# Third cross-attention of a perceiver: the first group's keys made in gaps of the stages ahead and kept, variances from whole squares, wider weighing in the second

## The chip, the cores and the metric

The kernel runs on one NeuronCore of a Trainium2 chip. Its engines are TensorE (PE in the profile: matmuls, with PEld for its weight loads), VectorE (DVE), ScalarE (ACT), GpSimd (POOL) and SyncE (SP, which issues loads). Each works through its own queue in order; semaphores tie them together. Arrays lie in SBUF, results of matmuls in PSUM, which has 8 banks of 128 x 512 f32. The metric is the device time of one execution in microseconds (us), the median of a few.

## What is computed

A chain of twelve stages (0 to 11) on a latent `x` of 64 x 256 and a context of 6272 x 256: four rounds of cross-attention, self-attention and a feed-forward or expert layer, each added to `x`. Three stages matter here. Stage 3 (L1 cross-attention, integer-valued softmax weights), shortened:

```
q = _fq_sym(q * scale); k = _fq_sym(k); v = _fq_sym(v, axis=2)
attn = softmax(einsum('bhqd,bhkd->bhqk', q, k))        # 16 heads of 16
attn = _fq_unsigned(attn, axis=-1)                     # steps of max/255
out = einsum('bhqk,bhkd->bhqd', attn, v) @ Wp + bp
```

Stage 6 (L2 cross-attention, "the third"), shortened. `cond` is the context; 8 groups of keys of 128, 2 query heads for each:

```
ln_out = _ln(hidden_states, ln_w, ln_b)
q, k, v = fp8-rounded linears of ln_out;  q, k = _ln(q), _ln(k)
core = _gqa(q, k, v)                                   # over the 64 latents
qx = _ln(fp8-rounded linear of ln_out)
kx, vx = split(einsum('bsi,oi->bso', cond, w_kv_x))
kx = _ln(kx)                                           # per group, over 128
xout = _gqa(qx, kx, vx)                                # over the 6272 of cond
return fp8-rounded concat([core, xout]) @ wproj * scales
```

Stages 4 and 5 between them are a self-attention (16 heads of 16 over 64 latents) and a layer of 8 experts.

## The kernel before

Every engine has a function for each stage (`x1_tensor`, `x2_vector`, ...), and the order of its work is written out by hand; there is no scheduler. Where TensorE would wait, `busy(pe, n, b)` issues n matmuls of 128x512 in bf16 whose result nobody reads (line 500); tables `BUSY_NORM`, `BUSY_OUT`, `BUSY_MHA` say how many at which place.

**Stage 3** runs over 8 pairs of heads. For each, `scores` (L1845) writes four parts, VectorE copies them out with their maximum (L1930), ScalarE takes exponentials in 7 parts (L2008), TensorE turns each (`turn`, L1860: 7 transposes of 128x128 in bf16), ScalarE or VectorE copies the turned part (L1813), and TensorE multiplies it with the values (`weigh`, L1869: 7 matmuls of 128x32).

**Stage 4**: `mha_tensor` makes queries and keys (L640), turns them (L647), scores (L655), turns the probabilities in two halves (L666), and multiplies by the values (L674). ScalarE takes the two exponentials (L736) and copies the two halves (L739).

**Stage 6** begins with two norms and the fp8 rounding on VectorE. TensorE makes six blocks of heads (`block`, L2097), each in a bank of its own (0 to 5): block 0 and 1 the cross queries, 2 and 3 the core queries, 4 the core keys, 5 the core values. VectorE takes their moments (L2334) and normalises blocks 0 and 1 (L2347), ScalarE blocks 2 to 4 (L2591), TensorE turns each (`turn`, L2109), ScalarE scales them (L2598), and `constant` (L2115) makes a term of the scores. Then the 8 groups follow. The context is in 49 tiles of 128, 13 chunks of up to 4 tiles. For each chunk of a group: `keys` (L2153: the group's weights as stationary operand, 512 columns of context moving, 2 matmuls); ScalarE copies the keys (L2630) and squares them (L2637); VectorE takes from the square its high bf16 half, which leaves a low half (`low_half`, L2385); `variance` sums both over 128 rows, a column per tile, with 8 bf16 matmuls (L2165, L2166); VectorE reads it out (L2396), GpSimd takes the power -1/2 (L2717); `scores` (L2182) multiplies keys and query; VectorE scales by the inverse and adds the constant (L2408), and keeps a running maximum (L2420). In `step(scored, weighed, ahead)` one group is scored while the group before is weighed (`weigh`, L2192), and `change` stands between two steps: it takes the maximum over lanes and rows (`turn_top` L2199, `spread_top` L2204) and begins the next group's keys. The first step, `step(0, None, 1, ...)`, has nothing to weigh; the core attention (L2123, L2133, L2141 on TensorE; L2482 to L2490 on VectorE) is put between its chunks.

The context is reloaded for it by SyncE: `ctxT` (feature-major, for the keys) in two halves during and behind stage 3's scores, `ctxN` (row-major, for the weighing) behind stage 3, into the buffer `vals`. In stage 3 the upper half of `vals`, named `back`, holds the scores of every other pair.

## Time and profile before

| | us |
|---|---|
| median of 3 runs | 1125.19 (1125.15 to 1125.84) |
| the profiled execution | 1126.49, of which span 1124.7 |
| TensorE busy | 1032.3 (92%) |
| VectorE, ScalarE, GpSimd busy | 745.1, 400.2, 158.5 |
| stage 3, from its norm to the end of its projection | 296 to 413 |
| stage 4 | 414 to 432 |
| stage 5 | 433 to 458 |
| stage 6, norms and head | 458 to 491 |
| its six blocks: start of the first, start of the third | 465.75, 469.2 |
| stage 6, first group scored | 491 to 530 |
| first weighing of stage 6 | 539.90 |
| load of `ctxN`, from issue to landing | 23.1 |
| GpSimd's power -1/2, 128x4 elements | 1.32 |
| VectorE's wait for the query projection, start of stage 3 | 2.04 |
| granted clock in 396 to 400, 400 to 415, 415 to 418 | 0.83, 0.50, 0.88 |
| granted clock in 473.5 to 477.5, and in 528.5 to 535 | 0.57, 0.50 |

How to read it: the rows further down are lines of the profile. A row of time has its start, its length, the engine, the line of the kernel, what is written and read, and in brackets how long the engine had waited and for whom. Matmuls overlap in the pipeline, so the time that one costs in a stream is read from start to start. f32 matmuls appear as two records each.

### The profile page before, as it was taken

The page shows a single profiled execution, that of the slowest core. Times are in us where ns is not written, and L with a number is a line of the kernel's source. Part 1 is how long each engine was busy: PE and PEld are TensorE (multiplying, and loading weights), DVE is VectorE, ACT ScalarE, POOL GpSimd, SP SyncE. Part 2 cuts the span into 40 slices and gives each one's busy share as a digit, 9 for nine tenths or more (in the row PEclk, how much of TensorE's full clock was granted, in tenths as well). Part 3 has the DMA queues.
Part 4 walks back from the last instruction along what each step waited for, and adds up shares of the span by engine and source line. Part 5 has one row for each costly group of instructions (what it writes and reads, how often), then busy time and mean ns, then how long its engine had stood idle before and what let it go on. Part 6 is the DMA issues. An engine that isn't in the chain of part 4 may idle for free.

```text
span 1124.7 us, 22087 instructions
## 1 busy us (share of the span) xinstructions
PE 1032.3 (92%) x8292; PEld 685.0 (61%) x8308; DVE 745.1 (66%) x1957; ACT 400.2 (36%) x738; POOL 158.5 (14%) x148
## 2 busy tenths in 40 slices
PE   6999999998777778899999999999999998988888
PEld 4667766664345545355676767777777776744444
DVE  4767676777678835658677676767676767553244
ACT  1333333334279951053333333333333333111203
POOL 0000000001000010124232223222232222000000
PEclk9999999999989969998999999999999998989899
DMA  7101010011302057640000000000000001323430
GB/s 271 37 21 37 19 37 19 23 47 54 122 1 117 2 202 259 229 141 1 1 1 2 1 0 0 0 0 1 0 0 0 0 1 59 108 79 129 158 116 3
DMA packets 17962, 64.51 MB, mean 57 GB/s; under 512 B 1392, under 2 KB 8304, under 8 KB 14448
## 3 DMA queue, kind: packets, MB, share of 16 engines
q1 hardware_dynamic: 17472, 63.08, 15.7%
q8 instruction: 39, 0.64, 0.2%
q10 hardware_dynamic: 432, 0.64, 0.2%
q14 instruction: 19, 0.16, 0.0%
HBM read 63.65 MB, written 0.07 MB: 57 GB/s over the span
## 4 chain that ended last, share of the span: by engine, by line
PE 71%; DVE 12%; issue 8%; ACT 4%; POOL 3%; DMA 1%; SPq 0%; DVEq 0%; POOLq 0%
PE ps L2192 14%; PE ps L2153 12%; PE ps L1460 7%; PE ps L2182 7%; PE ps L1450 4%; PE ps L1471 4%; PE ps L1494 2%; PE ps L1506 2%; POOL x_sum L2717 2%; PE ps L1845 2%; ACT wide L2008 1%; DVE S L2408 1%; DVE S L1930 1%; ACT x_keys L1813 1%; PE ps L500 1%
## 5 line engine op out<-in xcount | busy, mean ns | idle before, releaser
L2192 PE MATMUL ps<-vals,S 128*128 128x257 f32 x784 | 187.3, 382 | 0.7 <-ACT S L2642 0.7
L2153 PE MATMUL ps<-keysT,row_biases_sb 128*128 128x512 f32 (+1 forms) x416 | 187.2, 576 | 0.1
L2717 POOL TENSOR_TENSOR x_sum<-x_max,consts 128x4 f32<-128x4 f32 (+1 forms) x104 | 133.9, 1287 | 325.1 <-DVE x_max L2396 325.1
L2408 DVE SCALAR_TENSOR_TENSOR S<-ps,x_sum,keysT 128x128 f32<-128x128 f32 x392 | 110.9, 344 | 72.6 <-PE ps L2192 64.2
L2192 PEld LDWEIGHTS ps<-vals,S 128*128 128x128 f32 x784 | 142.4, 191 | 18.6 <-issue 1.0
L2642 ACT ACTIVATE S<-S 128x512 f32<-128x512 f32 (+1 forms) x104 | 62.7, 606 | 219.4 <-DVE S L2443 218.8
L2182 PE MATMUL ps<-x_q,x_keys 128*128 128x128 f32 x784 | 113.2, 286 | 0.0
L2153 PEld LDWEIGHTS ps<-keysT,row_biases_sb 128*128 128x128 f32 x416 | 77.0, 193 | 57.2 <-issue 52.1
L2182 PEld LDWEIGHTS ps<-x_q,x_keys 128*128 128x128 f32 x784 | 95.6, 191 | 0.0
L1460 PE MATMUL ps<-ring,S 128*128 128x512 f32 x196 | 92.2, 593 | 1.9 <-DVE ps L1601 1.9
L2630 ACT COPY x_keys<-ps 128x512 f32<-128x512 f32 (+1 forms) x104 | 57.1, 549 | 66.0 <-PE ps L2182 34.2
L1574 ACT ACTIVATE S<-ps 128x2048 f32<-128x2048 f32 (+1 forms) x25 | 46.1, 1843 | 83.6 <-PE ps L1506 76.1
L2385 DVE TENSOR_TENSOR sw_key_out<-wide 128x512 bf16<-128x512 f32 (+1 forms) x104 | 67.8, 652 | 3.9 <-ACT wide L2637 3.9
L500 PE MATMUL ps<-consts 128*128 128x512 bf16 x258 | 66.5, 391 | 4.1 <-PE ps L587 1.4
L2443 DVE TENSOR_TENSOR S<-S,xnT 128x512 f32<-128x512 f32 (+1 forms) x104 | 66.7, 654 | 0.3
L2420 DVE TENSOR_TENSOR wide<-wide,S 128x512 f32<-128x512 f32 x96 | 63.3, 659 | 0.3
L2637 ACT ACTIVATE wide<-ps 128x512 f32<-128x512 f32 (+1 forms) x104 | 60.0, 577 | 0.0
L1450 PE MATMUL ps<-S,ring 128*128 128x256 f32 (+1 forms) x200 | 50.3, 396 | 7.4 <-DMA S<-ctxT 6.7
L531 POOL TENSOR_TENSOR rstd<-var_eps,consts 64x1 f32<-64x1 f32 x14 | 7.7, 548 | 350.1 <-DVE var_eps L517 350.1
L1622 DVE TENSOR_SCALAR S<-ps,mask_sb 128x256 f32<-128x256 f32 x49 | 23.7, 484 | 46.0 <-PE ps L1460 42.8
L1460 PEld LDWEIGHTS ps<-ring,S 128*128 128x128 f32 x196 | 35.3, 190 | 26.9 <-issue 25.7
L2396 DVE TENSOR_SCALAR x_max<-ps 128x4 f32<-128x4 f32 (+1 forms) x104 | 16.5, 159 | 51.6 <-PE ps L2166 51.5
(444 smaller groups left out, 1520.9 us busy)
## 6 DMA issues: line engine op xcount, KB each, us to landing
ring<-weights SPq DMA_DIRECT2D x24, 1024.0 KB, 4.9
keysT<-ctxT SPq DMA_DIRECT2D x2, 3136.0 KB, 10.2
vals<-ctxN SPq DMA_DIRECT2D x1, 6272.0 KB, 23.1
S<-ctxT SPq DMA_DIRECT2D x12, 512.0 KB, 3.9
keysT<-weights SPq DMA_DIRECT2D x6, 864.0 KB, 9.9
ring<-weights SPq DMA_DIRECT2D x6, 768.0 KB, 7.0
ring<-weights SPq DMA_DIRECT2D x2, 864.0 KB, 5.4
row_biases_sb<-row_biases SPq DMA_DIRECT2D x1, 1416.0 KB, 12.1
```

Source lines behind the costliest of these rows:

```text
L500: pe.matmul(ps[:, b, :], product[:, 0:128], moving, start=True, stop=True)
L1450: ins = pe.matmul(ps[:, sw_keys_bank, TWO * o:TWO * o + n * TILE], w[:, 256 * k + 128 * o:256 * k + 128 * o + 128], sw_ctxT[ph][:, k, TWO ...
L1460: ins = pe.matmul(bank(sw_vk_bank), sw_ctxT[ph][:, k, a:a + TILE], w[:, 512 + 768 * k:1024 + 768 * k], start=k == 0, stop=k == KT - 1)
L2153: ins = pe.matmul(ps[:, c % 3, 0:width(c)], x2_wk[:, k, :], ctxT[:, k, span(c)], start=k == 0, stop=k == KT - 1)
L2182: ins = pe.matmul(ps[:, 3 + c % 2, 128 * s:128 * s + 128], x2_keys[:, c % 2, TILE * s:TILE * s + TILE], x2_q[:, :], start=True, stop=True)
L2192: ins = pe.matmul(bank(6, D + 1), S[:, a:a + TILE], ctx_and_ones[:, SUB * c + s, :], start=c == 0 and s == 0, stop=c == NC - 1 and s == su ...
L2385: dve.tensor_tensor(x2_low[c % 2][:, 0:width(c)], x2_dev[:, c % 2, 0:width(c)], high_half(c), ALU.subtract)\
L2408: ins = dve.scalar_tensor_tensor(S[:, a:a + TILE], ps[:, 3 + c % 2, 128 * s:128 * s + 128], x2_inv[:, c % 2, s:s + 1], x2_tile_const, ALU. ...
L2420: ins = dve.tensor_tensor(best, best, S[:, span(c)], ALU.max)
L2443: dve.tensor_tensor(chunk, chunk, spread(x2_top, 1, subs(c)), ALU.subtract).then_inc(sem("x2_shifted"), 1)
L2642: act.activation(chunk, chunk, ACT.Exp, scale=SCALE2).then_inc(sem("x2_exp"), 1)
L2717: pool.tensor_tensor(x2_inv[:, c % 2, 0:n], x2_var[:, c % 2, 0:n], C("neg_half").broadcast_to([128, n]), ALU.pow)\
```

## The change

1. **Stage 3**: `weigh` multiplies with 128 columns of values (four pairs' heads) in place of the 32 it needs; `finish` takes its 32 of them.
2. **First group's keys**: a new function `first_keys(pe, c)` makes chunk c of group 0's keys, and `copy_first_keys(act, c)` copies it into `x2_first_keys`, which is `back`, where all 13 chunks stay. Their weights are loaded at the start of the kernel, and VectorE subtracts their means at the start of stage 3. Chunk 0 stands behind stage 4's queries and keys, 1 and 2 ahead of the two turns of its probabilities, 3 ahead of stage 5's norm, 4, 5 and 6 around stage 6's norms, 7 to 12 between the blocks. The fillers at these places go.
3. **Variances of group 0 from whole squares**: `first_square` on ScalarE squares the kept keys, `first_variance` multiplies the f32 square by one f32 column; no high and low halves. VectorE reads the variances of 2 or 3 chunks at once, GpSimd takes powers of 8 or 9 columns.
4. **Order of the head**: blocks, turns, keys, variances and scores of group 0 are interleaved. Blocks use banks 0 and 1 in turn, so block i waits for the normalisation of block i-2. The core attention stands between the last scores.
5. **Loads**: `ctxN` is reloaded in two parts, since `back` is in use: tiles 0 to 23 as before, tiles 24 to 48 behind the last scores of group 0. GpSimd's ones, written into the same buffer, are split in the same way.

TensorE in stage 4, from the scores to the output product, before (`ps<-consts` is filler, L666 the two turns of probabilities):

```order
L655 MATMUL ps<-S 128x256 [waits mha_keys_ready]
L655 MATMUL ps<-S 128x256
L500 MATMUL ps<-consts 128x512 x4
L666 MATMUL ps<-consts,S 128x128 [waits mha_exp_ready]
L666 MATMUL ps<-consts,S 128x128
L500 MATMUL ps<-consts 128x512 x4
L666 MATMUL ps<-consts,S 128x128 [waits mha_exp_ready]
L666 MATMUL ps<-consts,S 128x128
L674 MATMUL ps<-S 64x32 [waits mha_probsT_ready,mha_values_ready]
```

and now (L2080 is `first_keys`, L673 the turns):

```order
L660 MATMUL ps<-S 128x256 [waits mha_keys_ready]
L660 MATMUL ps<-S 128x256
L2080 MATMUL ps<-keysT,x_first_wk 128x512 x2
L673 MATMUL ps<-consts,S 128x128 [waits mha_exp_ready]
L673 MATMUL ps<-consts,S 128x128
L2080 MATMUL ps<-keysT,x_first_wk 128x512 [waits x2_keys_ready]
L2080 MATMUL ps<-keysT,x_first_wk 128x512
L673 MATMUL ps<-consts,S 128x128 [waits mha_exp_ready]
L673 MATMUL ps<-consts,S 128x128
L681 MATMUL ps<-S 64x32 [waits mha_probsT_ready,mha_values_ready]
```

Each chunk of keys has taken the place of four fillers.

ScalarE at the same place now (L743 the exponentials, L750 the copies of the turned probabilities, L2085 the copies of the kept keys; before, it was the two exponentials and then the two copies, with nothing between):

```order
L743 ACTIVATE S<-S 128x256 [waits mha_shifted]
L2085 COPY vals<-ps 128x512 [waits x2_keys_psum]
L743 ACTIVATE S<-S 128x256 [waits mha_shifted]
L750 COPY S<-ps 128x256 [waits mha_probsT_psum]
L2085 COPY vals<-ps 128x512 [waits x2_keys_psum]
L750 COPY S<-ps 128x256 [waits mha_probsT_psum]
```

A copy of keys stands ahead of the second exponential and another ahead of the second copy.

TensorE at the head of stage 6, before, blocks 0 to 3 (L2097 blocks, L2109 turns):

```order
L2097 MATMUL ps<-ring,S 64x512 [waits weights_in0,rounded]
L2097 MATMUL ps<-ring,S 64x512 x3
L2097 MATMUL ps<-ring,S 64x512 [waits weights_in1]
L2097 MATMUL ps<-ring,S 64x512 x3
L2097 MATMUL ps<-ring,S 64x512 [waits rounded,weights_in2]
L2097 MATMUL ps<-ring,S 64x512 x3
L2109 MATMUL ps<-consts,S 128x128 [waits x2_block_normed]
L2109 MATMUL ps<-consts,S 128x128 x3
L2097 MATMUL ps<-ring,S 64x512 [waits weights_in3]
```

and now (L2146 blocks, L2160 turns, L2080 keys, L2334 variances), from block 1 to block 3:

```order
L2146 MATMUL ps<-ring,S 64x512 [waits weights_in1]
L2146 MATMUL ps<-ring,S 64x512 x3
L2080 MATMUL ps<-keysT,x_first_wk 128x512 [waits x2_keys_ready]
L2080 MATMUL ps<-keysT,x_first_wk 128x512
L2146 MATMUL ps<-ring,S 64x512 [waits x2_block_normed,rounded,weights_in2]
L2146 MATMUL ps<-ring,S 64x512 x3
L2160 MATMUL ps<-consts,S 128x128 [waits x2_block_normed]
L2160 MATMUL ps<-consts,S 128x128 x3
L2334 MATMUL ps<-consts,wide 128x1 [waits x2_squared]
L2334 MATMUL ps<-consts,wide 128x1 x3
L2146 MATMUL ps<-ring,S 64x512 [waits x2_block_normed,weights_in3]
```

Block 2 has got a wait for a normalisation, keys and a variance have come between the blocks.

The diff, cut to its core:

```diff
-        BUSY_OUT = {0: (8, 3), 1: (2, 5), 4: (2, 5), 7: (2, 5), 9: (2, 5)}
-        BUSY_MHA = {1: (4, 4, 4), 4: (8, 4, 4), 7: (12, 5, 5), 8: (4, 4, 4)}
+        FIRST_KEYS = {("qkv", 4): (0,), ("scores", 4): (1, 2), ("norm", 5): (3,), ("norm", 6.5): (4, 5)}
+        BUSY_MHA = {1: (4, 4, 4), 4: (0, 4, 0), 7: (12, 5, 5), 8: (4, 4, 4)}
...
-                    ins = pe.matmul(ps[:, 6 + j % 2, 0:32], x1_probsT[n % 2][:, s, :], vals_int[:, x1_tile(GROUP * e + s), 32 * j:32 * j + 32],
+                    ins = pe.matmul(ps[:, 6 + j % 2, 0:128], x1_probsT[n % 2][:, s, :], vals_int[:, x1_tile(GROUP * e + s), 128 * (j // 4):128 * (j // 4) + 128],
...
+            dve.wait_ge(sem("first_wk_in"), 16)
+            link(dve, "dve", dve.tensor_reduce(x2_wk_mean, x2_first_wk, AX, ALU.add))
+            link(dve, "dve", dve.tensor_scalar(x2_wk_mean, x2_wk_mean, 1.0 / GD, None, ALU.mult))
+            dve.tensor_tensor(x2_first_wk, x2_first_wk, spread(x2_wk_mean, 2, GD), ALU.subtract).then_inc(sem("x2_wk_ready"), 1)
...
+        def first_keys(pe, c):
+            if c >= 2:
+                pe.wait_ge(sem("x2_keys_ready"), c if c >= 8 else c - 1)
+            for k in range(KT):
+                ins = pe.matmul(ps[:, first_bank(c), 0:width(c)], x2_first_wk[:, k, :], ctxT[:, k, span(c)], start=k == 0, stop=k == KT - 1)
+            ins.then_inc(sem("x2_keys_psum"), 1)
+        def copy_first_keys(act, c):
+            act.wait_ge(sem("x2_keys_psum"), c + 1)
+            act.copy(x2_first_keys[:, span(c)], ps[:, first_bank(c), 0:width(c)]).then_inc(sem("x2_keys_ready"), 1)
...
+                if i >= 2:
+                    pe.wait_ge(sem("x2_block_normed"), i - 1)
-                        ins = pe.matmul(ps[rows_of(e), i, :], x2_in[:, which, k, :], heads[:, :, e, :], ...
+                        ins = pe.matmul(ps[rows_of(e), i % 2, :], x2_in[:, which, k, :], heads[:, :, e, :], ...
...
+            def first_variance(c):
+                pe.wait_ge(sem("x2_squared"), c + 1)
+                for s in range(subs(c)):
+                    a = SUB * c + s
+                    ins = pe.matmul(ps[:, 7, a:a + 1], x2_squares[c % 4][:, TILE * s:TILE * s + TILE], C("mean128")[:, 0:1], start=True, stop=True)
...
+            for c in range(10, NC):
+                first_variance(c)
+            core_scores()
+            first_scores(6)
+            first_scores(7)
+            first_scores(8)
+            core_turn()
+            first_scores(9)
+            first_scores(10)
+            core_out()
+            first_scores(11)
+            first_scores(12)
...
-            sp.dma_start(ctxN, io["ctxN"]).then_inc(sem("ctxN_in"), 16)
+            sp.dma_start(ctxN[:, 0:LOWER, :], io["ctxN"][:, 0:LOWER, :]).then_inc(sem("ctxN_in"), 16)
+        def reload_rest_of_ctxN(sp):
+            sp.wait_ge(sem("x2_scores_psum"), since("x2_scores_psum", NC))
+            sp.dma_start(ctxN[:, LOWER:, :], io["ctxN"][:, LOWER:, :]).then_inc(sem("ctxN_in"), 16)
```

On VectorE the first group's chunk is now `first_scale(c)` (the four scalings, then the running maximum), and the core softmax stands behind chunks 6 and 7, the next group's key weights behind chunk 9.

## Rows read from the trace of the kernel before

**Rows 1.** The page's head, and TensorE's granted clock in 40 slices (9: full).
```profile
span 1124.7 us, 22087 instructions
...
PEclk9999999999989969998999999999999998989899
```

**Rows 2.** A stretch: length, busy time by engine, granted clock, DMA share, GB/s.
```profile
400.00:415.00 15.00, 10.57 (x100) 7.54 (x102) 3.71 (x12) 9.36 (x16) 0.16 (x1) 0.50 0.26 96
```

**Rows 3.** TensorE in order of time, stage 3: turns L1860, weighings L1869.
```profile
394.39 0.34 PE L1869 MATMUL ps<-vals,x_keys 128*128 128x32 bf16 x7
394.58 0.55 PE L1860 MATMUL ps<-wide 128*128 128x128 bf16 x7
...
398.22 0.56 PE L1860 MATMUL ps<-wide 128*128 128x128 bf16 x7 [1.58 <-ACT wide L2008]
...
406.21 0.37 PE L1869 MATMUL ps<-vals,x_keys 128*128 128x32 bf16 x7 [0.98 <-ACT x_keys L1813]
406.42 0.91 PE L1860 MATMUL ps<-wide 128*128 128x128 bf16 x7
```

**Rows 4.** The chain that ended last, between two pairs: weighing, then scores.
```profile
354.79 0.34 PE ps L1869 x7
355.13 0.90 PE ps L1845 x8
```

**Rows 5.** TensorE: the same projection behind stage 3 and behind stage 4.
```profile
411.50 1.97 PE L587 MATMUL ps<-ring,attendedT 128*64 128x256 f32 x4 [0.36 <-ACT attendedT L596]
...
431.29 1.08 PE L587 MATMUL ps<-ring,attendedT 128*64 128x256 f32 x4 [0.36 <-ACT attendedT L596]
```

**Rows 6.** TensorE, stage 4: fillers behind the scores, second turn of probabilities.
```profile
426.04 1.03 PE L500 MATMUL ps<-consts 128*128 128x512 bf16 x4
...
428.47 0.44 PE L666 MATMUL ps<-consts,S 128*128 128x128 f32 x2
```

**Rows 7.** ScalarE, stage 4: the second copy of the turned probabilities.
```profile
428.94 0.37 ACT L739 COPY S<-ps 128x256 f32<-128x256 f32 x1 [0.27 <-PE ps L666]
```

**Rows 8.** VectorE, head of stage 6: normalisation of blocks 0 and 1.
```profile
471.88 2.63 DVE L2347 TENSOR_SCALAR S<-ps,S 128x128 f32<-128x128 f32 x8
```

**Rows 9.** TensorE, first group: keys, variance, scores, core scores; weight loads of core scores.
```profile
495.91 1.88 PE L2153 MATMUL ps<-keysT,row_biases_sb 128*128 128x512 f32 x4
497.63 0.17 PE L2165 MATMUL ps<-sw_value_part,wide 128*128 128x1 bf16 x1
...
497.84 1.14 PE L2182 MATMUL ps<-x_q,x_keys 128*128 128x128 f32 x8
498.81 1.90 PE L2123 MATMUL ps<-S 128*128 128x64 f32 x16
500.54 1.94 PE L2153 MATMUL ps<-keysT,row_biases_sb 128*128 128x512 f32 x4
...
L2123 PEld LDWEIGHTS ps<-S 128*128 128x128 f32 x16 | 1.9, 192 | 0.0
```

**Rows 10.** VectorE, first group: core maximum, scaling of a chunk, running maximum.
```profile
500.75 0.69 DVE L2482 TENSOR_REDUCE S<-ps 128x8 f32<-128x512 f32 x1 [1.36 <-PE ps L2123]
...
506.00 1.12 DVE L2408 SCALAR_TENSOR_TENSOR S<-ps,x_sum,keysT 128x128 f32<-128x128 f32 x4
507.04 0.15 DVE L2396 TENSOR_SCALAR x_max<-ps 128x4 f32<-128x4 f32 x1
507.16 0.69 DVE L2420 TENSOR_TENSOR wide<-wide,S 128x512 f32<-128x512 f32 x1
507.77 0.68 DVE L2385 TENSOR_TENSOR sw_key_out<-wide 128x512 bf16<-128x512 f32 x1
```

**Rows 11.** TensorE, from the first group to the second.
```profile
529.46 6.53 PE L2153 MATMUL ps<-keysT,row_biases_sb 128*128 128x512 f32 x8
535.83 0.27 PE L2199 MATMUL ps<-consts,attendedT 128*128 128x128 f32 x1
...
539.90 1.98 PE L2192 MATMUL ps<-vals,S 128*128 128x257 f32 x8 [0.69 <-ACT S L2642]
```

294 lines of the change are left out of this document (214 added, 80 removed).

## The prediction

> **What bounds the kernel now.** I read the row of granted clocks first [rows 1]: the kernel is on one core, TensorE is near 2.4 GHz nearly everywhere and busy 92% of the span, so an edit pays only where TensorE or what it waits for is the end of a chain. Three stretches matter. (a) Second cross-attention, 300 to 410 us: the chain of waits passes through VectorE, ScalarE and TensorE in turn, and between two pairs of heads it goes through one weighing straight into the next scores [rows 4]. (b) The self-attention behind it, 416 to 431 us: short steps, each waiting for the one before, with filler matmuls in the gaps. (c) The head of the third cross-attention and its first group, 462 to 540 us: one chunk of keys after another at TensorE's pace. At full clock a chunk costs 1.72 (keys, 495.91 to 497.63) + 0.21 (variance) + 0.97 (scores) = 2.90 us [rows 9]. At three places of these stretches TensorE runs at its lower level, 1.2 GHz, for some microseconds: 400 to 415 us [rows 2], and, as the table says, about 475 and 530. Each time it had stood waiting before.
>
> **The change part by part.** All against the profiled execution, 1126.49 us (span 1124.7 [rows 1], 1.8 us lie around it); the median of the runs shown, 1125.19, is 1.3 us lower, and I add the difference found to that.
>
> 1, *wider weighing in the second cross-attention*. Seven narrow weighings are 0.34 us long, seven turns of 128 columns 0.55 [rows 3]. With 128 columns a weighing becomes what a turn is: +0.21 each, 56 of them. Most stand beside ScalarE's exponentials and cost nothing. Where the weighing lies on the chain ahead of the next scores [rows 4] it costs its 0.21: once per pair of heads in six pairs, +1.3 us. At the lower level the two lengths are 0.37 and 0.91, +0.54 [rows 3]; I add one such, +0.5, for a slow stretch at the stage's start. Together **+1.8**.
>
> 2, *what that does to the clock*. The last pair has no scores left; TensorE waits for exponentials, and from 400 to 415 us its clock is at the lower level [rows 2]. At the lower level the projection behind the stage takes 1.97 us, at the full one 1.08 [rows 5]. With weighings twice as long TensorE stands less. If the clock stays up, the last turns and weighings save about 0.3 and the projection 0.9: **-1.2**. If it does not, the three weighings that follow ScalarE's last copies (the first at 406.21) cost +0.5 each, **+1.5** instead. I take -1.2: the fall came behind a wait of 1.58 us at 398.22 [rows 3], and in the slices from 337 to 394 us [rows 1], with exponentials waited for too but scores between them, there was none.
> The Trainium skill speaks against it: "TensorE: Matmul & The Clock Gate", section "Part 4: PE-mode transpose", says of the matmul in transpose mode that the clock's full level does not engage for it. By that rule the tail, half of whose work is turns, would stay slow, and this term would be +1.5 instead of -1.2; the trace, where the turn of 394.58 us ran at the full level [rows 3] with scores not far ahead of it, does not settle it.
>
> 3, *first keys of the weights on VectorE* (reduce, scale, subtract of 128x256 at the start of stage 3): about 1.0 us by an estimate from 0.69 for 512 columns [rows 10]. VectorE waits 2.04 us there for the query projection (table): **0**.
>
> 4, *keys 0 to 2 in the self-attention*. A chunk of keys takes 1.72 us, as the 8 fillers do that keys 0 replaces (1.03 for 4 overlapping ones [rows 6]): 0. But keys 1 and 2 are not as short as the gaps. Fillers started at 426.04 and the second turn of probabilities at 428.47 [rows 6]. Now TensorE does keys 1 (to 427.7), turn, keys 2 (to 429.7), turn: 1.2 us later. On ScalarE the copy of keys 2, which waits for them (429.85), stands ahead of the second copy of the probabilities; that began at 428.94 [rows 7] and now begins at 430.35. The output product waits for it: **+1.4**. Keys 3 (for 8 fillers), keys 4 and 5 (3.44 us for 3.19 of filler, with 0.9 us of waiting behind it) and keys 6 (1.72 for 2.1) cost 0; the added waits on copied keys are met by then, and behind them in the queue stands nothing that is ready earlier.
>
> 5, *the head of the third cross-attention*. Blocks 0 and 1 start at 465.75 (table) as before. Block 2 now writes bank 0 again and so waits for block 0's normalisation, which ends at 473.2 (half of the 2.63 us from 471.88) [rows 8]; it stood at 469.2 before (table). Keys 7 fill half of that. From 473.2 TensorE's queue holds: 4 blocks at 1.75 = 7.0 (two took 3.45, table); keys 8 to 12, 7.3; five turns, 2.2, and two constants, 1.8, by their lengths in the trace (a turn of 4 products 0.44 from start to start, a constant 0.9); 49 variance products; scores 0 to 5, 5.8; core scores 1.73 (498.81 to 500.54) [rows 9].
> *The variance product* is new: whole squares as f32 weights, one column moving, 49 of them, for 98 bf16 ones. The nearest row is the core scores, f32 weights of 128x128 with 64 columns moving: 1.73 us for 8, so 0.216 each, which their weight loads set [rows 9]. So 0.86 per chunk for 0.21, 10.6 us in all. Lower bound 0.13 each (6.4 us); upper, if no load overlaps, 2 x 0.19 = 0.38 (18.6 us). I take 0.216, the same load in the same form.
> Sum 7.0+7.3+2.2+1.8+10.6+5.8+1.7 = 36.4, plus 1.2 for the lower clock that followed the same wait before (0.57 from 473.5 to 477.5, table), plus 1.1 for a wait of block 5 on ScalarE's normalisation: core scores end at 511.9. VectorE keeps up until there, since it no longer takes low halves (0.61 us a chunk). *Then VectorE is the end*. Chunk 6 is scored by 513.0; for VectorE a chunk is 1.04 (scaling) + 0.61 (running maximum) + about 0.1 between them [rows 10], so 6 whole chunks 10.7, the short one 0.55, core softmax 1.4 + 1.65 (four pieces like the 0.69 [rows 10], a reciprocal), key weights 0.97 and lanes' top 0.65 by estimates from the same pieces: 15.9, to 528.9. And TensorE meets the turn of the core probabilities ahead of scores 9: it waits from 515.2 to 519.5, the clock falls, and some 1.7 us of that reach VectorE. Group 1's first keys need 3.44 us behind the last scores, so the turn of the tops starts at about 530.8 where it did at 535.83; from it to the first weighing it takes 4.07 us [rows 11], so 534.9 for 539.90: **-5.0**. Before, 528.5 to 535 ran at the lower level (table), and two chunks' keys there took 6.4 us from start to start [rows 11]; at full clock they are 3.44, and that is part of this gain.
>
> 6, *loads*. SyncE reloads half of the values' source where it did all, so weights behind it land earlier; nothing waited for them. The other half waits for the last first-group scores (527 us), lands some 12 us later (half of the table's 23.1), and is wanted at chunk 6 of the weighing, about 28 us after 534.9: 0. GpSimd's second memset stands before group 1's inverses and waits for the same scores: 0.
>
> Sum: +1.8 - 1.2 + 1.4 - 5.0 = **-3.0 us**, so 1125.2 - 3.0 = 1122.2. The groups 1 to 7 are untouched.
>
> **Rivals.** *A, the clock is not held* in the tail of the second cross-attention: term 2 becomes +1.5, the sum -0.3, 1124.9. For it: turns are half the work there, and each stretch is short. Against: TensorE has twice the weighing. *B, the clock is better than I say*: no fall at the normalisation wait (1.7 us won) and none at the core turn (1.5): -6.2, 1119.0. For it: the queue is fuller after 473. Against: a wait of 4.3 us is the longest in this stage. *C, slower: f32 weight loads with a single column moving do not overlap*. Place: TensorE's queue from 473 to 512. The profile gives 0.19 us as one load's length and 0.108 as its pace [rows 9]; at 0.19 the 98 loads (two per product) cost 8.1 us more, the sum is +5.1, 1130.3. It decides from 0.16 us a load upward. For it: no long product hides the load here. Against: core scores hide none either. *D, the keys don't fit their gaps at all*: ScalarE's copies, in order, hold up norms and softmax at 435, 460 and 463 too. Each would cost under 0.6 us (one copy), so +1.5: 1123.7, inside the range.
>
> **How the numbers follow.** Forecast 1122.2, with its own range 1120.5 to 1124.2 (variance product, weighing on the chain, VectorE's gaps, D): 0.45. A 0.27, B 0.15, C 0.10, others 0.03. A timing of this kernel can tell 0.2%, 2.25 us, from no change: faster means under 1122.9. That is two thirds of the forecast and B, some 0.48; slower is C and the rest, 0.13; the same 0.39. The range takes in B's lower edge and A's upper one, and leaves out C: 1118.3 to 1126.0.
>
> **What would show it.** Granted clock 1.0 from 400 to 410 us (term 2) or 0.5 (A). Seven weighings in 0.40 us at full clock. The second copy of the probabilities 1.4 us later within the self-attention. Block 2 behind block 0's normalisation; variance products at 0.22 us each (C: 0.38); TensorE waiting about 4 us ahead of the core turn; VectorE busy without gaps behind chunk 6; the first weighing of group 0 about 5 us nearer to the start of the stage's blocks. It is wrong if ScalarE or VectorE, not TensorE, paces 473 to 512, or if chunks wait for GpSimd's powers of 8 columns, which no row prices (4 columns take 1.32 us, table; between 1.3 and 2.6, hidden in either case by my schedule).

## The result

The changed kernel is slower by 0.3%: 1129.98 us (median of 20 runs, 1125.6 to 1133.31) beside 1126.87 for the kernel before in the same comparison (20 runs, 1123.14 to 1131.85), a ratio of 1.003 with a 95% interval of 1.0018 to 1.0042. The forecast was 3 us less, the measurement is some 3 us more; it lies outside the range of 1118.3 to 1126.0. Single runs of either kernel differ by up to 9 us, more than the whole effect, so the profiles are compared by stretches and not by their spans. The profiled execution of the changed kernel took 1133.31 us, the slowest of its 20.

A stretch goes from the start of one record of TensorE to that of the next one named. The second profile of before ("again") is of an unchanged copy.

| stretch, us | before | again | changed | forecast |
|---|---|---|---|---|
| to stage 3's first scores | 304.4 | 306.7 | 306.7 | same |
| first to last scores of stage 3 | 89.64 | 89.61 | 92.36 | +1.8 |
| to its output projection | 17.43 | 17.43 | 17.21 | -1.2 |
| to the turn of stage 4's norm | 5.18 | 5.15 | 6.05 | (in the -1.2) |
| to stage 4's output product | 12.16 | 12.15 | 13.79 | +1.4 |
| to stage 5's first expert | 9.09 | 9.10 | 9.36 | 0 |
| to stage 6's first block | 27.82 | 27.84 | 29.51 | 0 |
| to the core scores | 33.06 | 33.08 | 43.99 | 44.4 |
| to the turn of the tops | 37.02 | 36.98 | 22.43 | 20.6 |
| to the first weighing | 4.07 | 4.08 | 4.13 | 4.07 |
| to stage 6's projection | 432.19 | 432.15 | 432.85 | 0 |
| to the end of the span | 152.6 | 152.6 | 153.1 | 0 |

The stretches of the two profiles of before agree within 0.04 us from stage 3 on. They are a finer scale than the times, but they scatter too. The kernel a_order below has the instructions of the changed kernel up to the core scores of stage 6, and in its profile the scores of stage 3 take 90.60 us for 92.36, and the step from the projection to the turn of stage 4's norm 4.79 for 6.05. In both places the profiles differ in how long the granted clock is low. A difference of 1 or 2 us between two single profiles is therefore not yet the edit's.

The page's head of the changed kernel, which answers to [rows 1]:

```profile
span 1131.5 us, 21930 instructions
...
PEclk9999999999989989998999999999999998999899
```

The granted clock of the changed kernel in windows (length, busy time by engine, clock in the third number from the end), which answer to [rows 2]:

```profile
406.00:409.40 3.40, 3.24 (x35) 2.94 (x34) 0.78 (x2) 3.40 (x8) 0.00 (x0) 0.57 0.67 288
409.40:416.00 6.60, 3.69 (x53) 2.83 (x50) 1.77 (x6) 4.55 (x8) 0.00 (x0) 0.98 0.01 2
416.00:423.00 7.00, 6.32 (x15) 2.20 (x15) 1.56 (x5) 0.44 (x2) 2.88 (x6) 0.53 0.50 171
447.00:450.20 3.20, 3.20 (x9) 1.70 (x8) 1.62 (x9) 0.22 (x1) 0.00 (x0) 0.55 0.67 272
518.70:525.40 6.70, 6.70 (x34) 6.70 (x34) 1.08 (x5) 0.00 (x0) 1.79 (x1) 0.53 0.45 159
```

The one slow stretch of 15 us behind stage 3 is broken up, as hoped: 3.4 us, then full clock for 6.6 us. But the clock falls again at 416, right behind the weighings, and the projection at 416.28 and the fillers behind it are slow once more. Two stretches are at the lower level that were not before: 447 to 450 in the experts, and 518 to 525 at the core scores. One of before is gone: at stage 6's block 2 the clock does not fall.

TensorE, stage 4 of the changed kernel, which answers to [rows 6], and ScalarE beside it, which answers to [rows 7] (L2080 keys, L2085 their copies, L673 turns, L681 output product, L750 copies of the turns):

```profile
432.15 1.88 PE L2080 MATMUL ps<-keysT,x_first_wk 128*128 128x512 f32 x4
433.87 0.38 PE L673 MATMUL ps<-consts,S 128*128 128x128 f32 x2
434.09 1.88 PE L2080 MATMUL ps<-keysT,x_first_wk 128*128 128x512 f32 x4
435.81 0.38 PE L673 MATMUL ps<-consts,S 128*128 128x128 f32 x2
436.12 0.65 PE L681 MATMUL ps<-S 128*64 128x32 f32 x8
436.92 0.65 PE L681 MATMUL ps<-S 128*64 128x32 f32 x8
```

```profile
436.01 0.59 ACT L2085 COPY vals<-ps 128x512 f32<-128x512 f32 x1 [0.77 <-PE ps L2080]
436.49 0.38 ACT L750 COPY S<-ps 128x256 f32<-128x256 f32 x1
```

From the start of the first keys to the second copy it is 4.34 us (432.15 to 436.49); before, the same two points, the first filler and the copy, lay 2.90 apart (426.04 to 428.94). That is the +1.4 of the forecast. It is not all: the second half of the output product now waits for that copy (436.92), 0.80 us behind the first half; before, both halves went in one stream (TensorE):

```profile
428.84 1.18 PE L674 MATMUL ps<-S 128*64 128x32 f32 x16
```

This is the 0.27 us that the table has between the output product and the first expert. From the projection behind it (431.29 before, 438.84 now) to the first expert it is 6.64 us in both kernels, so keys 3 cost nothing there.

TensorE in the head of stage 6, which answers to [rows 9] and [rows 11] (L2146 block 2, L2334 variance products, L2174 core scores, L2345 scores, L2184 core turn):

```profile
482.62 1.94 PE L2146 MATMUL ps<-ring,S 128*64 128x512 f32 x8 [2.07 <-DVE S L2447]
...
510.40 1.84 PE L2334 MATMUL ps<-consts,x_keys 128*128 128x1 f32 x16
512.11 1.14 PE L2345 MATMUL ps<-x_q,vals 128*128 128x128 f32 x8
...
518.98 3.65 PE L2174 MATMUL ps<-S 128*128 128x64 f32 x16
522.43 4.40 PE L2345 MATMUL ps<-x_q,vals 128*128 128x128 f32 x24
531.03 0.66 PE L2184 MATMUL ps<-consts,x_keys 128*128 128x128 f32 x4 [4.21 <-DVE x_keys L2610]
```

Block 2 waits 2.07 us for block 0's normalisation, as forecast. Eight variance products take 1.71 us (510.40 to 512.11), 0.214 each; 0.216 was taken. The core turn is waited for 4.21 us. New is that the core scores take 3.45 us for 1.73, at the lower clock.

VectorE there, which answers to [rows 10]:

```profile
519.16 0.17 DVE L2517 TENSOR_SCALAR x_first_var<-ps 128x9 f32<-128x9 f32 x1 [0.46 <-PE ps L2334]
524.49 1.12 DVE L2527 SCALAR_TENSOR_TENSOR S<-ps,x_first_inv,keysT 128x128 f32<-128x128 f32 x4 [5.16 <-PE ps L2345]
525.65 0.69 DVE L2540 TENSOR_TENSOR wide<-wide,S 128x512 f32<-128x512 f32 x1
```

VectorE stands 5.16 us for scores 6, which are queued behind the last variances and the core scores; from then on it is busy to the end of the group but for 0.49 us.

### The profile page after: what moved, and what is told of

Its sections match the earlier page's. It is cut to its first block, busy times and chain, and to the rows that moved or that the text cites. A ratio compares the mean times of both kernels' runs of the same rounds, so it can differ in the third digit from the quotient of the medians.

```text
span 1131.5 us, 21930 instructions
## 1 busy us (share of the span) xinstructions
PE 1047.6 (93%) x8259; PEld 705.2 (62%) x8259; DVE 737.3 (65%) x1937; ACT 401.6 (35%) x738; POOL 149.7 (13%) x142
## 4 chain that ended last, share of the span: by engine, by line
PE 74%; DVE 13%; issue 6%; ACT 4%; POOL 1%; DMA 1%; SPq 0%; DVEq 0%; POOLq 0%
PE ps L2246 14%; PE ps L2204 11%; PE ps L1475 7%; PE ps L2233 7%; PE ps L1465 4%; PE ps L1486 4%; PE ps L1509 2%; PE ps L1860 2%; PE ps L1521 2%; ACT wide L2027 2%; DVE S L2508 1%; DVE S L1949 1%; PE ps L2943 1%; PE ps L2080 1%; ACT x_keys L1828 1%
## 5 line engine op out<-in xcount | busy, mean ns | idle before, releaser
L2204 PE MATMUL ps<-keysT,row_biases_sb 128*128 128x512 f32 (+1 forms) x364 | 160.9, 568 | 0.0
L2880 POOL TENSOR_TENSOR x_sum<-x_max,consts 128x4 f32<-128x4 f32 (+1 forms) x91 | 115.4, 1268 | 296.4 <-DVE x_max L2496 296.4
L2508 DVE SCALAR_TENSOR_TENSOR S<-ps,x_sum,keysT 128x128 f32<-128x128 f32 x343 | 97.0, 344 | 68.3 <-PE ps L2246 64.2
L2233 PE MATMUL ps<-x_q,x_keys 128*128 128x128 f32 x686 | 98.8, 286 | 0.0
L2204 PEld LDWEIGHTS ps<-keysT,row_biases_sb 128*128 128x128 f32 x364 | 67.3, 190 | 48.2 <-issue 43.6
L2233 PEld LDWEIGHTS ps<-x_q,x_keys 128*128 128x128 f32 x686 | 83.5, 191 | 0.0
L500 PE MATMUL ps<-consts 128*128 128x512 bf16 x225 | 58.6, 397 | 1.7 <-PE ps L2284 0.2
L2485 DVE TENSOR_TENSOR sw_key_out<-wide 128x512 bf16<-128x512 f32 (+1 forms) x91 | 59.3, 651 | 0.0
L1475 PEld LDWEIGHTS ps<-ring,S 128*128 128x128 f32 x196 | 35.8, 193 | 27.1 <-issue 25.8
L2785 ACT ACTIVATE wide<-ps 128x512 f32<-128x512 f32 (+1 forms) x91 | 52.5, 576 | 0.0
L1486 PEld LDWEIGHTS ps<-ring,S 128*128 128x128 f32 x196 | 37.7, 192 | 16.3 <-issue 12.5
## 6 DMA issues: line engine op xcount, KB each, us to landing
vals<-ctxN SPq DMA_DIRECT2D x1, 3200.0 KB, 12.1
```

The costliest lines, as they stand in the source:

```text
L1475: ins = pe.matmul(bank(sw_vk_bank), sw_ctxT[ph][:, k, a:a + TILE], w[:, 512 + 768 * k:1024 + 768 * k], start=k == 0, stop=k == KT - 1)
L1486: ins = pe.matmul(ps[0:TILE, sw_v1_bank, D * s:D * s + D], sw_ctxT[ph][:, k, a:a + TILE], w[:, 1024 + 768 * k:1280 + 768 * k], start=k == ...
L2204: ins = pe.matmul(ps[:, c % 3, 0:width(c)], x2_wk[:, k, :], ctxT[:, k, span(c)], start=k == 0, stop=k == KT - 1)
L2233: ins = pe.matmul(ps[:, 3 + c % 2, 128 * s:128 * s + 128], x2_keys[:, c % 2, TILE * s:TILE * s + TILE], x2_q[:, :], start=True, stop=True)
L2485: dve.tensor_tensor(x2_low[c % 2][:, 0:width(c)], x2_dev[:, c % 2, 0:width(c)], high_half(c), ALU.subtract)\
L2508: ins = dve.scalar_tensor_tensor(S[:, a:a + TILE], ps[:, 3 + c % 2, 128 * s:128 * s + 128], x2_inv[:, c % 2, s:s + 1], x2_tile_const, ALU. ...
```

## The experiments

Each ratio is against the kernel before, measured beside it on the same chip. Stretches of the profiles stand in one table behind the experiments.

**One part alone: the wide weighing in the kernel before (b_wide).**

```diff
-ps[:, 6 + j % 2, 0:32], ..., vals_int[:, x1_tile(GROUP * e + s), 32 * j:32 * j + 32],
+ps[:, 6 + j % 2, 0:128], ..., vals_int[:, x1_tile(GROUP * e + s), 128 * (j // 4):128 * (j // 4) + 128],
```

> The kernel before with one part of the change alone: the weighings of the second cross-attention take 128 columns in place of 32, and the take of the result its own 32 of them. Theory S (size): the wide weighing is the mis-sized term; in the profile of the changed kernel the stage has grown by 2.9 us up to 400 us, not by 1.8, and the clock in its tail is held in part only, so this kernel is 2 to 3 us slower than before (1.002 to 1.003). Rival H (hidden): the wide weighings lie beside ScalarE's exponentials, the growth came from elsewhere (keys' weights, reloads), and the time is as before within 0.5 us. A second rival, K (clock): the clock is held through the tail and the output projection, the time is 0 to 1 us under before.

Measured: 1127.03 us, 1.0009 (0.9987 to 1.0031). The interval holds all three expectations, so the time decides nothing; the profile shows scores of stage 3 in 92.38 us for 89.64, but also 29.19 for 27.82 in the experts, where nothing was changed.

**The opposite: narrow weighings in the changed kernel (a_narrow).** The two lines of the diff above, taken back.

> The changed kernel with narrow weighings and nothing else. Theory W (the wide weighing costs what its stage shows): 2 us under the changed kernel, 1 us over before (1.001). Rival C (its place in the clock's falls matters as much): with narrow ones the clock falls in the tail of the second cross-attention and at the wait of the third's block 2, which takes back what the stage gains; as the changed kernel, 1.002 to 1.003.

Measured: 1128.81 us, 1.0026 (1.0016 to 1.0035). The changed kernel has 1.003. W's 1.001 lies outside the interval and C's 1.002 to 1.003 in it: the wide weighing is worth nothing measurable here. What narrow ones save in length they seem to lose to the clock. The granted clock over a whole execution was 0.971 to 0.974 in the ten runs of this kernel and 0.975 to 0.980 in the twenty of the changed one. Its profile shows one place (TensorE, the wait ahead of block 2, and the granted clock over it):

```profile
479.92 3.37 PE L2146 MATMUL ps<-ring,S 128*64 128x512 f32 x8 [2.08 <-DVE S L2447]
483.22 0.87 PE L2160 MATMUL ps<-consts,S 128*128 128x128 f32 x4
```

```profile
479.50:483.50 4.00, 3.58 (x10) 1.12 (x11) 1.55 (x5) 0.00 (x0) 0.10 (x1) 0.60 0.27 68
```

Block 2 takes 3.30 us for the 1.87 of the changed kernel, behind the same wait of 2.1 us. The loss that the forecast put at 1.2 us came up in this profile and not in that of the changed kernel. It is not the narrow weighing alone that decides it: with wide ones and the keys in their gaps the clock falls there in two of six profiles, a_order and a_order2, whose edits stand behind block 2. TensorE in a_order, where the next row starts at 481.95:

```profile
479.00 3.02 PE L2146 MATMUL ps<-ring,S 128*64 128x512 f32 x8 [2.08 <-DVE S L2449]
```

With narrow ones it falls in four of four. Where keys 4 to 6 fill the wait (a_move and the kernels built on it, below), it does not fall in any of three.

**The load of the key weights put later (a_wklate)**, behind the first cross-attention's loads:

```diff
-            sp.dma_start(x2_first_wk, ...).then_inc(sem("first_wk_in"), 16)
             if sweep:
                 SWEEP_LOADS[1](sp)
+            sp.dma_start(x2_first_wk, ...).then_inc(sem("first_wk_in"), 16)
```

> The changed kernel with the load of the first group's key weights put behind the loads of the first cross-attention in SyncE's queue, not at the start. Theory L (load): the 128 KB in 256 rows of 512 bytes at the start delay the first tiles of the context, which TensorE waits for; that was 2.0 to 2.3 us at 15 us in the profile, so this kernel is about 2 us faster than the changed one, that is 1 to 1.5 us slower than before. Rival N (noise of the start): executions differ there anyway; the time stays that of the changed kernel, about 3.4 us (1.003) over before.

Measured: 1127.89 us, 1.0017 (1.0000 to 1.0034); the interval holds both L and N. The profile speaks for N: stage 3's scores begin at 307.7 us, no earlier than in the changed kernel, and the unchanged copy of before began them at 306.7 as well.

**The price of the variance product (a_high, a_bf16sq).** The upper bf16 half of each square alone (the lower halves are left out):

```diff
-x2_squares[c % 4][:, TILE * s:TILE * s + TILE], C("mean128")[:, 0:1],
+x2_squares[c % 4].bitcast(BF16).rearrange("p (n h) -> p n h", h=2)[:, TILE * s:TILE * s + TILE, 1], C("mean128")[:, 0:1].bitcast(BF16)[:, 1:2],
```

> The changed kernel with the variance products of the first group taking only the upper bf16 half of each square as weights (the lower halves are left out): 49 bf16 loads in place of 98 f32 ones. Theory P (price of the variance product): the f32 loads cost 10.6 us of TensorE's queue between the norms and the core scores, and the run of them ahead of the core scores brings the fall of the clock to the lower level there (518.7 to 525.4 us); without them the first group ends 5 to 7 us earlier, so 1.5 to 3.5 us under before. Rival V (VectorE is the end): VectorE's 16 us from chunk 6 on and its moments of the blocks ahead of that hold the end, and only the 5.2 us in which it stood still at chunk 6 can be won in part: 2 to 3 us under the changed kernel.

Measured: 1120.78 us, 0.9945 (0.9924 to 0.9966). That is 6.2 us under before by the ratio, more than P's 1.5 to 3.5. The same with squares that ScalarE writes as rounded bf16:

```diff
-act.activation(x2_squares[c % 4][:, 0:width(c)], x2_first_keys[:, span(c)], ACT.Square)
+act.activation(x2_squares[c % 4].bitcast(BF16)[:, 0:width(c)], x2_first_keys[:, span(c)], ACT.Square)
```

> The changed kernel with the squares of the first group written by ScalarE as rounded bf16 and taken as such by the variance products (49 bf16 loads, nothing left out but the digits below bf16 of each square). Theory P (price of the f32 variance product): the head, from the first block to the first weighing, takes 62.6 us as it did with the upper halves alone, and the time is 5 to 7 us under before. Rival R: ScalarE's write of bf16, or its place in the queue, costs something that the upper halves did not, and the head stays over 65 us.

Measured: 1120.57 us, 0.9947 (0.9929 to 0.9965). Both profiles have 62.65 and 62.63 us from the first block to the first weighing, for 70.55. TensorE with rounded squares, the end of the first group:

```profile
510.27 0.34 PE L2334 MATMUL ps<-consts,wide 128*128 128x1 bf16 x8
510.47 1.14 PE L2345 MATMUL ps<-x_q,vals 128*128 128x128 f32 x8
511.44 0.34 PE L2334 MATMUL ps<-consts,x_keys 128*128 128x1 bf16 x8
511.65 0.16 PE L2334 MATMUL ps<-consts,wide 128*128 128x1 bf16 x1
511.67 1.98 PE L2174 MATMUL ps<-S 128*128 128x64 f32 x16
```

```profile
511.00:520.00 9.00, 5.65 (x55) 5.26 (x53) 7.16 (x19) 1.07 (x3) 3.32 (x2) 1.00 0.34 117
521.00:527.50 6.50, 6.31 (x36) 5.97 (x37) 5.21 (x17) 0.58 (x1) 0.00 (x0) 0.52 0.01 3
```

Eight bf16 products take 0.20 us (510.27 to 510.47) for 1.71. The core scores are at the full level now, and the fall comes later, in the wait of 4.21 us for the core turn. So the f32 products cost 7.9 us of the head, 0.16 each for 49, and the earlier fall goes with them. P holds: the second experiment came out as said (62.6 us, some 6 us under before), the first gained more than P's 5 to 7 us in the head.

**The order of the end of the first group (a_order, a_order2).** Core scores ahead of scores 6, variances 10 to 12 between scores (TensorE's part of the edit below); VectorE reads them behind chunk 7 and takes the core softmax one chunk later:

```diff
             first_scores(5)
-            for c in range(10, NC):
-                first_variance(c)
             core_scores()
             first_scores(6)
+            first_variance(10)
             first_scores(7)
+            first_variance(11)
+            first_variance(12)
             first_scores(8)
```

> The changed kernel with the end of the first group in another order: the core scores and scores 6 and 7 ahead of the variances of chunks 10 to 12, VectorE's last reading of variances behind the scaling of chunk 7. Theory V (VectorE is the end): VectorE stood still for 5.2 us ahead of chunk 6 and was then busy to the end of the group, so what it does earlier is gained: 3 to 4 us less than the changed kernel, about the time of before. Rival T (TensorE is the end): the same products in another order end at the same time, and the gain is under 1 us. In either case the core turn waits less on TensorE or not at all.

Measured: 1129.06 us, 1.002 (1.0001 to 1.0039). The stand of 5.16 us is gone and the gain is under 1 us all the same: T's number, but not its reason, since TensorE does not end at the same time, it waits. The expectation that the core turn would wait less was wrong in both. VectorE and TensorE in its profile:

```profile
525.20 0.69 DVE L2612 TENSOR_TENSOR x_keys<-x_keys,x_small 128x512 f32<-128x512 f32 x1
528.80 1.12 DVE L2529 SCALAR_TENSOR_TENSOR S<-ps,x_first_inv,keysT 128x128 f32<-128x128 f32 x4 [2.92 <-PE ps L2345]
```

```profile
525.94 1.12 PE L2184 MATMUL ps<-consts,x_keys 128*128 128x128 f32 x4 [4.65 <-DVE x_keys L2612]
526.85 3.41 PE L2345 MATMUL ps<-x_q,vals 128*128 128x128 f32 x15
```

Scores 9 are queued behind the core turn: TensorE stands 4.65 us for it (4.21 in the changed kernel), its clock falls, and VectorE stands 2.92 us for scores 9. A wait has taken the place of the one removed. So scores 9 and 10 were put ahead of the turn:

```diff
             first_scores(8)
-            core_turn()
             first_scores(9)
             first_scores(10)
+            core_turn()
+            first_scores(11)
             core_out()
-            first_scores(11)
```

> The changed kernel with the other order of the end of the first group (core scores ahead of scores 6, variances of chunks 10 to 12 between the scores) and, besides, scores 9 and 10 ahead of the turn of the core probabilities. In the order before this one VectorE's stand of 5.2 us ahead of chunk 6 was gone, but it stood 2.9 us for scores 9, which were queued behind the turn. Theory Q (queue): with scores 9 and 10 ahead of the turn VectorE does not wait there, and the head takes 66.5 to 67.5 us for 69.8. Rival C (clock): TensorE still stands before the turn, its clock falls as before, and the head gains under 1 us.

Measured: 1125.31 us, 0.9989 (0.9974 to 1.0004): the time of before, with f32 squares and all else of the change. From the core scores to the turn of the tops it is 19.33 us for 22.33 in the order before. Q's mechanism holds: TensorE waits 1.13 us ahead of the turn, VectorE not at all, and the clock does not fall there. Its number was missed, since 1.6 us of the gain went into a longer fall of the clock behind the wait ahead of block 2 (44.90 us to the core scores for 43.30), so the head is 68.4 us for the expected 67. This profile is of the slowest of its 12 runs (1130.74 us).

**Narrow weighings and bf16 squares, with the second order (a_best1) and without (a_bn).** The edits are those shown above.

> The changed kernel with narrow weighings again, bf16 squares, and the new order of the end of the first group with scores 9 and 10 ahead of the turn. Theory: the parts add up: bf16 squares 8 us, the order up to 3 us (less here, since VectorE had less of a stand), narrow weighings 1 to 2.7 us; the time is 9 to 12 us under before. Rival V: with cheap variances VectorE paces the end and the order gives nothing; 7 to 9 us under before.

Measured: 1121.42 us, 0.9957 (0.994 to 0.9974). No more than bf16 squares alone gave: the order gives 0.4 us where variances are cheap (20.30 us for 20.70 at the end), and the head has the fall at block 2 (39.21 for 37.79). Neither expectation held; the parts don't add up.

> The changed kernel with bf16 squares in the first group and narrow weighings in the second cross-attention. With wide ones seven profiles took 90.6 to 92.7 us (mean 92.0) for its scores, with narrow ones 89.6 to 89.7 in three. Theory W (the wide weighing costs what the profiles say): 1.5 to 2.5 us less than bf16 squares alone, 6 to 7.5 us under before (0.9935 to 0.9945), and 17.4 us in the tail for 17.2. Rival C: what narrow weighings save there is lost to the clock in the tail, and the time is that of bf16 squares alone (0.9947).

Measured, narrow weighings and bf16 squares: 1122.91 us, 0.9975 (0.9964 to 0.9987), slower than with wide ones (0.9947). W falls here, and C did not go far enough. Against the 1.9 us won in the scores of stage 3 stand 1.6 us at block 2, where the clock falls again (39.44 us for 37.79), and 2 us in the last stages (151.3 for 149.4), where nothing was changed.

**Keys 1 to 3 out of stages 4 and 5 (a_move)**, with bf16 squares and narrow weighings. The fillers of before stand in their places again; of the edit:

```diff
-        FIRST_KEYS = {("qkv", 4): (0,), ("scores", 4): (1, 2), ("norm", 5): (3,), ("norm", 6.5): (4, 5)}
+        FIRST_KEYS = {("qkv", 4): (0,), ("norm", 6.5): (1, 2)}
...
             block(0)
+            first_keys(pe, 4)
             block(1)
+            first_keys(pe, 5)
+            first_keys(pe, 6)
             first_keys(pe, 7)
```

> The kernel with bf16 squares and narrow weighings, and keys 1 to 3 taken out of the self-attention and the experts' start, with the filler matmuls of before back in their places; keys 1 to 3 stand around the norms of the third cross-attention and keys 4 to 6 between its first two blocks and the third. Theory G (the gaps are too short for keys): the self-attention takes 12.2 us for 13.7, the step behind it 9.1 for 9.4, the experts 27.8 for 29.5 if the fall of the clock there belongs to keys 3, and the head grows by 1 to 3 us, since 2.1 us of the wait ahead of block 2 are there to be filled: 0 to 2 us less than bf16 squares with narrow weighings. Rival H (the head pays in full): three chunks at 1.72 us are 5.2 us, and the kernel is 1.5 to 2 us slower than that one.

Measured: 1120.42 us, 0.9949 (0.9932 to 0.9966); 2.5 us less than the same with keys in the gaps (G had said 0 to 2). G holds: 12.54 us for 13.69 in the self-attention, 9.10 for 9.37, 27.80 for 29.46 in the experts, and 41.15 for 39.44 in the head. Over stages 4 and 5, from 430 to 465 us, its clock does not fall:

```profile
430.00:465.00 35.00, 30.47 (x153) 17.12 (x151) 16.98 (x54) 5.50 (x17) 1.71 (x4) 1.00 0.53 187
```

**bf16 squares in every group (b_bf16, a_bf16all, a_move_all, a_move_all_w).** Since TensorE paces groups 1 to 7 too, cheap variances were tried there, first in the kernel before:

```diff
-                    pe.matmul(ps[:, 7, a:a + 1], high_half(c)[:, tile_of], x2_mean, start=True, stop=False)
-                    ins = pe.matmul(ps[:, 7, a:a + 1], x2_low[c % 2][:, tile_of], x2_mean, start=False, stop=True)
+                    ins = pe.matmul(ps[:, 7, a:a + 1], x2_dev[:, c % 2, :].bitcast(BF16)[:, tile_of], x2_mean, start=True, stop=True)
```

> The kernel before with bf16 squares in all 8 groups and nothing else of the change: 4 variance products a chunk in place of 8, no lower halves on VectorE (the digits below bf16 of each square are left out). Theory T (TensorE's queue paces groups 1 to 7): 4 loads of 0.025 us less in each of 104 chunks, 10 us under before (0.991). Rival N: the loads of the lower halves lie beside the drain of the product before and cost nothing; within 2 us of before.

Measured: 1115.39 us, 0.9901 (0.9883 to 0.9919): T. TensorE, a chunk of its first group:

```profile
497.42 0.24 PE L2165 MATMUL ps<-sw_value_part,wide 128*128 128x1 bf16 x4
497.52 1.14 PE L2181 MATMUL ps<-x_q,x_keys 128*128 128x128 f32 x8
```

0.10 us for the 0.21 of [rows 9]; the groups behind take 424.18 us for 432.19. Two things changed at once here, half the variance products and no low halves on VectorE; 0.11 us in each of the 91 chunks behind the first group would be 10 us by this price, and 8.0 are seen.

The same edit in the changed kernel, with its first group's squares in bf16 and narrow weighings:

> The changed kernel with narrow weighings and bf16 squares in all 8 groups. Theory: the first group's early keys and the cheap variances add up, 7 us (head) and 9 us (groups 1 to 7) under before: 0.985 to 0.987. Rival: if b_bf16 shows nothing in groups 1 to 7, this is the time of a_bn.

Measured: 1111.5 us, 0.9875 (0.9856 to 0.9895). With keys 1 to 3 moved as well:

> All findings together: bf16 squares in all 8 groups, narrow weighings, keys 1 to 3 out of the self-attention and the experts. Theory G: bf16 squares in all groups gave 1111.5 with early keys and keys 1 to 3 in the gaps; taking these out gave 2.5 us: 1108 to 1110, 0.984 to 0.986. Rival: the two do not add up, 0.9875 as without the moving.

Measured: 1112.46 us, 0.9887 (0.987 to 0.9904); the rival holds, the two don't add up. With wide weighings:

> The same with wide weighings. Theory W: 1.5 to 2.5 us slower than with narrow ones. Rival C: as fast as with narrow ones or faster, since its clock falls less in the tail (17.2 us for 17.4) and at block 2.

Measured: 1113.48 us, 0.9897 (0.988 to 0.9914), the same within their intervals, so neither W nor C is decided. These three are 12 to 14 us under before, and faster than both kernels, at the price that the squares have bf16 digits; 10 us of it are bf16 squares without any early keys. What the early keys add to these is 0.5 to 3 us, and the intervals overlap.

**The kernel before again (b_same).**

> The kernel before, unchanged, for a second profile. The experts' stage took 29.5 us in three of the four profiles with wide weighings and kept keys, and 29.2 with wide weighings alone, each with a stretch at the lower clock, and 27.8 in the one profile of before. Theory T (the change brings the fall): 27.8 again, and 89.6 us for the scores of the second cross-attention. Rival E (executions differ there anyway): a stretch at the lower clock can stand in the experts' stage of before too, or another length in the second cross-attention.

Its profile (1128.84 us) has before's stretches to 0.04 us except for the start, T. Two profiles do not show that executions of one kernel agree, though. In one comparison the kernel before ran 29 times, and by and large the longer it took, the lower was its granted clock (1122.78 us at 0.978, 1132.05 at 0.969; correlation -0.91). So falls of the clock come and go between executions of one kernel too; which of them do so, two profiles that agree can't show.

| stretch, us | wide alone | narrow, changed | bf16, wide | bf16, narrow | bf16, narrow, keys moved |
|---|---|---|---|---|---|
| scores of stage 3 | 92.38 | 90.53 | 91.63 | 89.78 | 89.75 |
| to projection and turn | 23.23 | 22.68 | 23.25 | 22.68 | 22.97 |
| stage 4 | 12.26 | 13.70 | 13.79 | 13.69 | 12.54 |
| to the experts | 9.09 | 9.37 | 9.36 | 9.37 | 9.10 |
| experts to first block | 29.19 | 29.49 | 29.50 | 29.46 | 27.80 |
| to core scores | 33.08 | 45.23 | 37.79 | 39.44 | 41.15 |
| to turn of tops | 36.89 | 22.83 | 20.70 | 20.55 | 20.55 |

## Why the prediction was wrong

Three steps failed, and each left out or misplaced a fall of TensorE's clock: that the clock stays up through the projection behind stage 3 (term 2), that keys put in place of fillers ahead of stage 5 cost nothing behind them (term 4), and that the core scores run at full clock (term 5).

**Term 1, the wide weighing: right in size.** Over the eight profiles with wide weighings the scores of stage 3 take 91.88 us on average (90.6 to 92.7), over nine with narrow ones 90.19 (89.6 to 91.4): +1.7 for +1.8. The one pair of profiles says +2.7. The rest is the clock at the stage's start: over its first 25 us it is 0.80 in the changed kernel and 0.86 before. Profiles with the same clock there differ by the weighing alone: at 0.80 wide ones take 92.3 to 92.7 us and narrow ones 90.5 to 90.6 (one, with a further fall later, 91.4), at 0.86 the one wide profile 91.6 and three narrow ones 89.6 to 89.8. That is 1.8 to 2.0 us. TensorE in the changed kernel, which answers to [rows 3]:

```profile
399.79 0.55 PE L1875 MATMUL ps<-wide 128*128 128x128 bf16 x7
400.18 0.55 PE L1884 MATMUL ps<-vals,x_keys 128*128 128x128 bf16 x7
400.57 0.55 PE L1875 MATMUL ps<-wide 128*128 128x128 bf16 x7
```

A wide weighing is a turn, 0.39 us from start to start, as said.

**Term 2, the clock: the mechanism in part, the value none.** -1.2 was forecast, since the clock would be held in the tail. It mostly is: from the last scores to the projection it is 0.88 to 1.00 in the eight profiles with wide weighings and 0.63 to 0.65 in the nine with narrow ones. But TensorE waits for ScalarE there, and this stretch takes 17.2 us for 17.4. Then, in all eight, the clock falls within 1 us of the projection's start: for 6.8 us in five of them (some 6.05 us from the projection to the turn of stage 4's norm, for 5.2 before) and for 3.4 in three (4.7 to 4.8). From the last scores to that turn it is 22.76 us on average with wide ones, 22.74 with narrow ones. The failed step is "if the clock stays up, the last turns and weighings save about 0.3 and the projection 0.9": the clock was taken as one state for the whole tail. Terms 1 and 2 together give +1.7 by stretches; by times a_narrow sets the two at 0.4 us, within the noise. The lower clock of the narrow kernel elsewhere, as at block 2, fits that.

**Term 4, keys in the self-attention: nearly right in stage 4, missed behind it.** +1.4 forecast, +1.6 measured (12.16 to 13.79), and 0.3 more behind it, where the second half of the output product waits for the late copy. The step "Keys 3 (for 8 fillers) ... cost 0" failed. It is right up to the first expert (6.64 us from the projection in both kernels), but in the experts 1.7 us are lost, where the clock falls to the lower level for some 3 us. It does so in nine of the ten profiles with keys 1 to 3 in those gaps, and in none of the three where they are moved; of the four without early keys it does so in the one with wide weighings. With keys moved the experts are back at 27.80. That the placement brings the fall is so shown by its frequency; what in it does so is not settled, since one kernel with keys there (a_wklate) has no fall and one without (b_wide) has it. Keys 1, 2 and 3 were only moved together, so the step that failed may be that of keys 1 and 2 as well.

**Term 5, the head: its queue nearly right, its end not.** The core scores were to start 44.4 us behind the first block (510.2 for 465.75) and do so after 43.99. Part of that is luck: 1.2 us of the 44.4 were for a fall at block 2 that this profile does not have. With the fall it takes 45.23 (a_narrow), so the queue itself was put some 0.8 us too short. The variance product was to cost 0.216 us and costs 0.214; rival C (0.38) is out. But from the core scores to the turn of the tops it is 22.43 us for the 20.6 forecast. The fall of the clock was put at the wait for the core turn. One came there (531.8 to 535.2), but another, from 518.1 to 525.0, came ahead of the core scores, behind 17 f32 variance products within 5.0 us (chunks 8 to 12, with scores 5 between them). So the core scores and scores 6 ran at the lower level, and VectorE stood 5.16 us there. The two other profiles with these products in this order, a_wklate and a_narrow, have that fall as well (from 516.3 and 517.8); the two that spread the last nine products between scores, a_order and a_order2, don't, nor do those with bf16 squares. The head gained 3.6 us for 5.0.

**Terms 3 and 6** are nothing, as forecast: there is no wait of TensorE for the reloaded half, which lands 12.1 us after its issue.

**The sum** by stretches, with averages where there are several profiles: 1.7 + 0.0 + 1.6 + 0.3 + 1.7 - 3.6 = +1.7 us, for +3.1 measured (interval 2.0 to 4.7, from the ratio's). Another 0.7 lies in stage 6's groups (432.85 for 432.19): 0.2 in the first weighing, 0.5 behind the last turn of tops, where the clock is at the lower level for 6.8 us in both kernels. The rest is not located; the last stages differ between profiles by over 4 us (148.5 to 153.1), with no order by edit.

**The rivals.** A, the clock is not held, gave 1124.9 with +1.5 for term 2; the clock was held, and the term is 0.0, halfway. B, a better clock, came true in its first half (no fall at block 2 in this profile) and not in its second. The forecast was not of one mind on it: term 5 has 1.2 us for block 2 and 1.7 for the core turn, B has 1.7 and 1.5. C is out. D, the keys don't fit their gaps, names the right places, but its mechanism, ScalarE's copies that hold up the norms behind stage 4 (+1.5), is not what came: they cost nothing up to the first expert, and from there to the first block a_wklate, which has the copies and no fall, takes 27.84 us for 27.82. The loss there came by the clock. A slower kernel was given 0.13. What I left out is that several places could each lose a microsecond or two to the clock, and that such losses have one sign where the forecast counts on full clock.

## What to carry to other kernels

Measure a gap before filling it with real work: keys of 1.72 us in gaps of 1.2 us (four fillers, 426.04 to 427.23) on a chain of short steps cost some 3 us, with the fall of the clock behind them, while three such chunks in and around a wait of 2.1 us elsewhere cost 1.7 us. Here a product with one moving column took 0.21 us with f32 weights of 128x128 and 0.025 with bf16 ones, so its price lies in the type of the stationary operand (8 us here in one group); in the kernel before, 4 bf16 products a chunk in place of 8, and no low halves, gave 10 us over all groups. A wait that is removed (VectorE's 5.2 us) shows its gain only when what is queued behind the next wait is moved too. And a price for a fall of the clock needs several profiles: here such falls came and went with no edit ahead of them.

## What the runs showed of the hardware

TensorE's clock fell with its queue full. In the changed kernel it went to the lower level at 518.1 us, when TensorE had not stood still for over 13 us (its last wait was 0.39 us, ahead of 504.49) and most of its work in the 5 us before had been one-column f32 products; with bf16 products in the same order it stayed at the full level from 511 to 520 (1.00) and fell in a wait. That the f32 products bring it is supported by three profiles with them in this order, which all have the fall, and by those without, which don't. I had expected falls behind waits alone.

The same wait of 2.1 us ahead of block 2 was followed by the lower level in six of ten profiles, among them a_order (block 2 in 2.95 us), and not in four, among them the changed kernel (1.87 us), though these two have the same instructions up to there. So a loss of 1.1 to 1.4 us came and went without an edit ahead of it, and single profiles of two kernels cannot tell it from an edit's own cost. All four profiles with narrow weighings have it and two of six with wide ones; whether the weighing, 80 us ahead, has a part in that is not shown.
